# Local attention's scores in 64x64 tiles, and four score products at once for the selected tokens

## The chip, the cores and the metric

The kernel is one program on one core of a Trainium2 chip. Its time is the device time of that core in microseconds, the median of the runs shown. TensorE (PE) multiplies, VectorE (DVE) and ScalarE (ACT) work on its results in PSUM, GpSimd (POOL) prepares small operands, SyncE (SP) issues DMAs.

## The reference

Six layers follow each other: a gated feed-forward layer, linear attention, the feed-forward layer again, a layer that joins local attention and attention of selected tokens ("route" below), latent attention, and the route layer once more. The change is in the route layer, which runs twice, on 8 batches of 256 tokens, 128 features, 8 heads of 64:

```python
light = local_attn(_ln(x), Wqkv, Wout_l)   # windows of 64 tokens; a window sees itself and its two neighbours
sim = jnp.where(valid, sim, -1e9)          # the first and the last window have one neighbour
sq, iq = route(x, rt_q, 64)                # the 64 best tokens of a batch as queries
skv, ikv = route(x, rt_kv, 128)            # the 128 best as keys
heavy = heavy_attn(x[iq], x[ikv], skv, ...)  # 8 heads over 128 keys and one null key with its null value
out = null_q everywhere, heavy at iq
return out + light
```

All matrix products are in float32, except small ones in bfloat16 that add a mask or a maximum.

## The kernel before, in words

Each engine has its own program, written out by hand, and semaphores join them. In the route layer a first part does local attention for all batches, with the router's iterations on DVE beside it, and a second part does the selected tokens.

**Local attention.** Batch b goes through four quarters, one for each pair of heads. The PE loop is a Python loop over b from -1 to 8 and written out in full. In each quarter PE does `turned_scores(b, pair)` (keys as rows, queries as columns, for the exponential by ACT), a projection of a later batch (`project_qk`), `scores(b + 1, pair)` (queries as rows, from which DVE takes the maximum in `top`), and the products with the values (`values`, `summed`) or `project_out`. A half h holds two windows. `scores` writes 128 queries x 192 keys for each half and each of the pair's two heads, with the 64 features of a head as contraction, so two heads stand above each other on PE's rows (64x128 tiles). A product with one row (`g_row`, `g_neg`) then adds -1e9 to the 64 columns that one of the two windows may not see. `turned_scores` does the same with keys and queries exchanged, and a bfloat16 product with `marks` adds the negative maximum and the mask. `scores(b, pair)` waits until DVE has taken the maximum of the pair before (`mx`), `turned_scores` until ACT has read the pair before (`p`). A projection waits until the one before last has been copied out of its bank (two banks, `input_bank`); q is copied by DVE, k and v by ACT. In a quarter DVE's queue has `normalised`, `copy_q` and `scale_z` where there is one, `top`, and up to four router steps, in this order.

**Selected tokens.** `heavy(b)` runs once for each batch; the six middle ones are a loop of the hardware over two bodies (`batches`). PE: `heavy_scores(b)`, `heavy_turn_out(b - 1)`, `gather(b + 1)`, `spread_slots(b)`, `heavy_project_out(b - 1)`, `heavy_turn(b)`, `project_k(b + 1)`, `put_back(b - 1)`, `project_q(b + 1)`, `heavy_values(b)`, `project_v(b + 1)`. `heavy_scores` takes all 128 rows: `h_q[j]` has zeros in the other head's rows. `heavy_values` does head side 0, then head side 1, each with a product of 4 rows that brings the null value in. DVE: `pick(b + 1)`, the maximum, `h_back` (a comparison of the spread slots with a row number), `pick_row`, copies, the reciprocal, `add_heavy(b - 1)`, `copy_heavy_q(b + 1)` in two halves, `token_stats(b - 1)`, and the product of values and reciprocal. `heavy_turn_out(b)` needs the latter (`ho`), and also ACT's copy of v (`hv`).

## Time and profile before

| | |
|---|---|
| median of 3 runs | 1091.48 us (1088.66 to 1154.73) |
| the profiled execution | 1089.49 us, span 1087.7 us |
| mean granted TensorE clock | 0.930 of 2.4 GHz |
| busy share of the span | PE 89%, PEld 64%, DVE 62%, ACT 35%, POOL 13% |
| chain that ended last | PE 70%, DVE 13%, issue 10%, ACT 4% |

The span runs from the first to the last instruction. A float32 product has two records of PE (it goes through the array twice), so x4 in a row is two products. A record's length counts from its start to its modelled end, some of it beside the next record, so the time of a block is read from one group's start to the next one's.

### The profile page before, as it was taken

How to read it: one execution, taken by the hardware profiler on the slowest of the kernel's cores; microseconds unless marked ns; L12 is line 12 of the kernel's file. 1: busy time of each engine (PE TensorE's matmuls, PEld its weight loads, DVE VectorE, ACT ScalarE, POOL GpSimd, SP SyncE). 2: the span in 40 equal slices, each digit the busy share in tenths (PEclk: the TensorE clock that was granted, in tenths of full speed). 3: DMA queues.
4: the chain of work that ended last, by engine and by line, in shares of the span. 5: the costliest groups of instructions: out<-in, count | busy, mean ns of one | idle time of the engine just before them, and what ended most of it. 6: DMA issues, size and time to landing. Idle time of an engine off the chain costs nothing.

```text
span 1087.7 us, 23083 instructions
## 1 busy us (share of the span) xinstructions
PE 966.8 (89%) x8840; PEld 698.3 (64%) x8840; DVE 670.0 (62%) x1914; ACT 381.5 (35%) x913; POOL 141.6 (13%) x289
## 2 busy tenths in 40 slices
PE   3499999899559999999999589999879999999997
PEld 3378888788446666667776245555446667667775
DVE  5778787887664565566555456667453665565553
ACT  3321111111333434333332136667623433333332
POOL 5011111110110000000000254350010000000000
PEclk9889898999689999999999569999979999999997
DMA  5000000000000000000000233322000000000000
GB/s 188 0 2 1 2 0 0 0 0 1 0 1 1 1 2 2 2 2 2 1 0 1 60 86 97 82 75 75 3 1 1 2 1 2 2 2 2 10 10 20
DMA packets 13751, 20.07 MB, mean 18 GB/s; under 512 B 1504, under 2 KB 12128, under 8 KB 12256
## 3 DMA queue, kind: packets, MB, share of 16 engines
q1 hardware_dynamic: 13520, 18.67, 5.9%
q8 instruction: 60, 0.98, 0.4%
q10 hardware_dynamic: 144, 0.20, 0.1%
q14 instruction: 27, 0.22, 0.1%
HBM read 14.53 MB, written 4.19 MB: 17 GB/s over the span
## 4 chain that ended last, share of the span: by engine, by line
PE 70%; DVE 13%; issue 10%; ACT 4%; POOL 2%; DVEq 1%; DMA 1%; SPq 0%; POOLq 0%; ACTq 0%
PE bank L1598 6%; PE bank L1659 6%; PE bank L1627 6%; PE bank L1645 5%; PE bank L1685 3%; PE bank L1605 3%; PE bank L604 3%; PE bank L1083 2%; PE bank L1833 2%; PE bank L1828 2%; PE bank L589 2%; PE bank L1104 2%; PE bank L1631 2%; PE bank L1117 2%; PE bank L1803 2%
## 5 line engine op out<-in xcount | busy, mean ns | idle before, releaser
L1398 DVE TENSOR_REDUCE arena<-bank 128x2 f32<-128x512 f32 x128 | 85.0, 688 | 53.3 <-PE bank L1083 52.2
L2166 DVE TENSOR_REDUCE arena<-bank 128x4 f32<-128x768 f32 x64 | 61.3, 958 | 65.6 <-PE bank L1631 65.6
L1221 ACT ACTIVATE arena<-bank 128x512 f32<-128x512 f32 x128 | 74.5, 594 | 51.0 <-PE bank L1104 50.2
L604 PE MATMUL bank<-arena 128*128 128x9 f32 x512 | 66.2, 257 | 13.4 <-DVE arena L929 7.5
L604 PEld LDWEIGHTS bank<-arena 128*128 128x128 f32 x512 | 65.6, 200 | 16.6 <-issue 8.7
L1627 PE MATMUL bank<-arena 64*128 64x192 f32 x512 | 76.2, 374 | 0.0
L1598 PE MATMUL bank<-arena,w_sb 128*128 128x256 f32 x256 | 74.5, 418 | 1.3 <-ACT arena L1924 1.3
L589 PE MATMUL bank<-arena 128*128 128x128 f32 x512 | 72.1, 289 | 0.3 <-DVE arena L863 0.3
L1945 ACT ACTIVATE arena<-bank 128x768 f32<-128x768 f32 x64 | 51.9, 811 | 55.8 <-PE bank L1649 54.1
L589 PEld LDWEIGHTS bank<-arena 128*128 128x128 f32 x512 | 67.1, 203 | 2.8 <-DVE arena L863 0.3
L1645 PE MATMUL bank<-arena 64*128 64x192 f32 x512 | 66.2, 356 | 0.4 <-ACT arena L1945 0.4
L1598 PEld LDWEIGHTS bank<-arena,w_sb 128*128 128x128 f32 x256 | 46.1, 199 | 19.3 <-issue 12.4
L1659 PE MATMUL bank<-arena 128*32 128x192 f32 (+2 forms) x1536 | 54.5, 274 | 1.2 <-DVE x L2181 1.2
L1083 PE MATMUL bank<-arena 72*128 72x256 bf16 x256 | 52.4, 291 | 1.1 <-DVE arena L1398 1.1
L1659 PEld LDWEIGHTS bank<-arena 128*32 128x32 f32 x1536 | 42.2, 109 | 17.1 <-issue 12.6
L2082 POOL TENSOR_TENSOR arena<-arena,c_sb 128x8 bf16<-128x8 f32 x32 | 9.1, 283 | 332.4 <-issue 295.4
L1645 PEld LDWEIGHTS bank<-arena 64*128 64x128 f32 x512 | 38.8, 185 | 21.0 <-issue 12.5
L1104 PE MATMUL bank<-arena 128*128 128x256 bf16 x256 | 49.5, 277 | 0.5 <-ACT arena L1221 0.4
L2137 DVE SCALAR_TENSOR_TENSOR arena<-arena,c_sb 16x256 f32<-16x256 f32 x98 | 46.2, 471 | 2.5
L1627 PEld LDWEIGHTS bank<-arena 64*128 64x128 f32 x512 | 38.5, 184 | 14.1 <-issue 7.3
L868 DVE TENSOR_TENSOR arena<-bank,c_sb 128x512 f32<-128x512 f32 x64 | 43.8, 684 | 2.8 <-PE bank L589 2.8
L1935 ACT ACTIVATE arena<-bank 128x512 f32<-128x512 f32 x32 | 19.1, 597 | 73.1 <-PE bank L1605 73.1
(297 smaller groups left out, 1978.4 us busy)
## 6 DMA issues: line engine op xcount, KB each, us to landing
arena<-q_dram SPq DMA_DIRECT2D x24, 192.0 KB
arena<-k_dram SPq DMA_DIRECT2D x24, 192.0 KB
w_sb<-w_dram SPq DMA_DIRECT2D x2, 1578.5 KB, 11.0
q_dram<-arena SPq DMA_DIRECT2D x24, 64.0 KB, 2.9
k_dram<-arena SPq DMA_DIRECT2D x24, 64.0 KB, 2.1
x<-x_dram SPq DMA_DIRECT2D x4, 256.0 KB, 4.4
out_dram<-x SPq DMA_DIRECT2D x4, 256.0 KB, 2.3
c_sb<-c_dram SPq DMA_DIRECT2D x1, 601.5 KB, 6.5
```

The source lines that it names most:

```text
L589: ins = pe.matmul(bank[1 + u % 2][:, j * P:(j + 1) * P], l_pkm[parity][:, quad * 4 + j, h * P:(h + 1) * P], l_pqT[parity][:, h * P:(h + 1) ...
L604: ins = pe.matmul(bank[7][:, h * 144 + k * LV:h * 144 + (k + 1) * LV], l_a[:, u % 2, j, :], l_v[parity][:, h * LH + k, :], start=u == 0 an ...
L1083: ins = pe.matmul(bank[s % 2][:, h * T:(h + 1) * T], a_stack[n % 3][0][0:STACK_ROWS, u, h * P:(h + 1) * P], a_stack[n % 3][1][0:STACK_ROWS ...
L1104: ins = pe.matmul(bank[2 + u % 2][:, k * T:(k + 1) * T], a_stack[b % 3][1][:, u, k * P:(k + 1) * P], a_stack[b % 3][0][:, u, :], start=Tru ...
L1221: act.activation(a_pT[:, u % (2 * GROUP), :, :].rearrange("p k t -> p (k t)"), bank[2 + u % 2][:, :], ACT.Exp).then_inc(S["p"], 1)
L1398: dve.tensor_reduce(a_mx[:, i % 2, :, u % GROUP], bank[s % 2][:, :].rearrange("p (h k) -> p h k", h=HALVES), AX_X, ALU.max, negate=True).t ...
L1598: ins = pe.matmul(to[:, j * T:(j + 1) * T], w_sb[:, at:at + P], g_zT[b % 2][:], start=True, stop=True)
L1627: pe.matmul(bank[j][:, h * KEYS:(h + 1) * KEYS], q[rows, pair, h * P:(h + 1) * P], k[rows, pair, h * WIN:h * WIN + KEYS], start=True, stop ...
L1645: pe.matmul(bank[2 + j][:, h * KEYS:(h + 1) * KEYS], k[rows, pair, h * P:(h + 1) * P], q[rows, pair, h * WIN:h * WIN + KEYS], start=True, ...
L1659: ins = pe.matmul(to[u * E_COLS:(u + 1) * E_COLS, out_at:out_at + n], stationary(h, u), g_p[:, 2 * s + u // 2, u % 2, h * KEYS + at:h * KE ...
L1945: act.activation(g_p[:, pair, :, :], two_banks(2)[:, :, 0:SPAN], ACT.Exp).then_inc(S["p"], 1)
L2166: dve.tensor_reduce(g_mx[:, s, :, :, i].rearrange("p h j -> p j h"), two_banks(0)[:, :, 0:SPAN].rearrange("p j (h k) -> p j h k", h=HALVES ...
```

## The change

Local attention: each product covers one window of 64 queries (or keys), and the keys (or queries) it may see, 128 or 192 columns. Windows go in the pairs (0, 3) and (2, 1), with both heads: four products on four 64x64 tiles of PE. The products for the mask are gone; `close_windows` has DVE write -1e9 once in a stage into the places in PSUM that no product writes. `scores(b + 1, pair)` stands directly behind `turned_scores(b, pair)`, ahead of the projections.

Selected tokens: `heavy_scores` takes 64 rows for each head, and in every second pair the heads change sides, so that the products of two successive pairs lie on the four different tiles. `heavy_values` alternates the sides, without the product for the null value; DVE multiplies the null values by their probabilities (`h_null`) and adds them. The slots of `h_back` come from two transposes in `gather` and no longer from `spread_slots`. The loop over batches is written out in full (`unrolled`) on PE, ACT and DVE. Fewer memsets on POOL (`FILLS` 5 for 16), and `marks` and `null_v` are smaller (192 and 256 columns less to load).

```diff
+        WINDOW_PAIRS = ((0, 3), (2, 1))
+
+        def window(n):
+            first, last = max(n - 1, 0) * WIN, min(n + 2, T // WIN) * WIN
+            h = n // 2
+            shift = h * KEYS - h * WIN
+            return slice((n % 2) * WIN, (n % 2 + 1) * WIN), slice(first + shift, last + shift), slice(first, last)
...
-                for h in range(HALVES):
-                    for j in range(2):
-                        rows = slice(j * DH, (j + 1) * DH)
-                        pe.matmul(bank[j][:, h * KEYS:(h + 1) * KEYS], q[rows, pair, h * P:(h + 1) * P],
-                                  k[rows, pair, h * WIN:h * WIN + KEYS], start=True, stop=False, skip_group_check=True)
-                    far = h * KEYS + (KEYS - WIN if h == 0 else 0)
-                    for j in range(2):
-                        ins = pe.matmul(bank[j][:, far:far + WIN], g_row[j * DH:j * DH + 1, h, :],
-                                        g_neg[j * DH:j * DH + 1, :], start=False, stop=True, skip_group_check=True)
+                for windows in WINDOW_PAIRS:
+                    for n in windows:
+                        for j in range(2):
+                            at, cols, seen = window(n)
+                            rows = slice(j * DH, (j + 1) * DH)
+                            ins = pe.matmul(bank[j][at, cols], q[rows, pair, n * WIN:(n + 1) * WIN], k[rows, pair, seen],
+                                            start=True, stop=True, skip_group_check=True)
                 ins.then_inc(S["sc_psum"], 1)
...
-                for h in range(HALVES):
-                    for j in range(2):
-                        rows = slice(j * DH, (j + 1) * DH)
-                        pe.matmul(bank[2 + j][:, h * KEYS:(h + 1) * KEYS], k[rows, pair, h * P:(h + 1) * P],
-                                  q[rows, pair, h * WIN:h * WIN + KEYS], start=True, stop=False, skip_group_check=True)
-                    for j in range(2):
-                        rows = slice(j * DH, (j + 1) * DH)
-                        ins = pe.matmul(bank[2 + j][:, h * KEYS:(h + 1) * KEYS], marks[rows, i, h, :],
-                                        g_mT[s][rows, h * WIN:h * WIN + KEYS], start=False, stop=True,
-                                        skip_group_check=True)
+                for windows in WINDOW_PAIRS:
+                    for n in windows:
+                        for j in range(2):
+                            at, cols, seen = window(n)
+                            rows = slice(j * DH, (j + 1) * DH)
+                            pe.matmul(bank[2 + j][at, cols], marks[rows, i, :], g_mT[s][rows, seen],
+                                      start=True, stop=False, skip_group_check=True)
+                    for n in windows:
+                        for j in range(2):
+                            at, cols, seen = window(n)
+                            rows = slice(j * DH, (j + 1) * DH)
+                            ins = pe.matmul(bank[2 + j][at, cols], k[rows, pair, n * WIN:(n + 1) * WIN], q[rows, pair, seen],
+                                            start=False, stop=True, skip_group_check=True)
                 ins.then_inc(S["st_psum"], 1)
...
                 if now:
                     turned_scores(b, 0)
                 if ahead:
-                    project_qk("q23", b + 1)
+                    scores(b + 1, 0)
                 if now:
                     turn_tops(b, 1)
                 if ahead:
-                    scores(b + 1, 0)
+                    project_qk("q23", b + 1)
...
                 for h in range(HALVES):
-                    ins = pe.matmul(bank[1][:, 0:NKV + NQ], h_y[:, h, :], h_hot[:, h, :],
+                    ins = pe.matmul(bank[1][:, 0:NKV + NQ], h_y[:, h, :], h_hot[:, h, 0:NKV + NQ],
                                     start=h == 0, stop=h == 1)
                 ins.then_inc(S["x_psum"], 1)
+                wait(pe, S["hback"], b)
+                for h in range(HALVES):
+                    ins = pe.transpose(bank[4][0:NQ + 1, h * P:(h + 1) * P], h_hot[:, h, NKV:NKV + NQ + 1], ident)
+                ins.then_inc(S["b_psum"], 1)
                 for h in range(HALVES):
                     ins = pe.matmul(bank[3][:, 0:1], h_hot[:, h, 0:NKV], h_w[:, h, :], start=h == 0, stop=h == 1)
                 ins.then_inc(S["w_psum"], 1)
-
-            def spread_slots(b):
-
-                pe.wait_ge(S["hslot"], b + 1)
-                wait(pe, S["hpT"], 2 * b)
-                pe.matmul(bank[4][0:NQ + 1, 0:T], c("ones", ROUTES)[:, 0:NQ + 1], h_slot[:], start=True, stop=True)\
-                  .then_inc(S["b_psum"], 1)
...
+            def side_of(t, side):
+                return side ^ (t % 2)
+
             def heavy_scores(b):
-                pe.wait_ge(S["kq"], 3 * b + 3)
+                pe.wait_ge(S["kq"], 2 * b + 2)
                 for t in range(PAIRS):
-                    for j in range(2):
-                        ins = pe.matmul(bank[5 + t // 2][j * NQ:(j + 1) * NQ, (t % 2) * 256:(t % 2) * 256 + NKV + 1],
-                                        h_q[j][:, t, :], h_k[:, t, :], start=True, stop=True)
+                    for side in range(2):
+                        half = side_of(t, side)
+                        rows = slice(half * DH, (half + 1) * DH)
+                        ins = pe.matmul(bank[5 + t % 2][side * NQ:(side + 1) * NQ, (t // 2) * 256:(t // 2) * 256 + NKV + 1],
+                                        h_q[rows, t, :], h_k[rows, t, :], start=True, stop=True, skip_group_check=True)
                 ins.then_inc(S["hs_psum"], 1)
             def heavy_turn(b):
                 pe.wait_ge(S["hp"], b + 1)
                 for t in range(PAIRS):
-                    pe.transpose(bank[0][:, t * P:(t + 1) * P], h_p[:, t, 0:NKV], ident)
-                pe.wait_ge(S["hback"], b + 1)
-                pe.transpose(bank[4][0:PAIRS, 0:P], h_p[:, :, NKV], ident).then_inc(S["hpT_psum"], 1)
+                    ins = pe.transpose(bank[0][:, t * P:(t + 1) * P], h_p[:, t, 0:NKV], ident)
+                ins.then_inc(S["hpT_psum"], 1)
             def heavy_values(b):
-                pe.wait_ge(S["hpT"], 2 * b + 2)
+                pe.wait_ge(S["hpT"], b + 1)
                 pe.wait_ge(S["hv"], b + 1)
                 wait(pe, S["x_done"], b)
-                for j in range(2):
-                    rows = slice(j * NQ, (j + 1) * NQ)
-
-                    pe.matmul(bank[7][rows, 0:PAIRS * DH], h_pn[:, rows],
-                              w("null_v", PAIRS)[:, j * 256:(j + 1) * 256], start=True, stop=False,
-                              skip_group_check=True, tile_position=(0, j * NQ))
-                    for t in range(PAIRS):
-                        head = 2 * t + j
+                for t in range(PAIRS):
+                    for side in range(2):
+                        rows = slice(side * NQ, (side + 1) * NQ)
+                        head = 2 * t + side_of(t, side)
                         ins = pe.matmul(bank[7][rows, t * DH:(t + 1) * DH], h_pT[:, t, rows],
-                                        h_v[:, head * DH:(head + 1) * DH], start=False, stop=True,
-                                        skip_group_check=True, tile_position=(0, j * NQ))
+                                        h_v[:, head * DH:(head + 1) * DH], start=True, stop=True,
+                                        skip_group_check=True, tile_position=(0, side * NQ))
                 ins.then_inc(S["ho_psum"], 1)
...
+            def close_windows(i):
+
+                for n in range(2):
+                    at = slice(n * WIN, (n + 1) * WIN)
+                    dve.tensor_scalar(two_banks(i)[at, :, P + n * WIN:P + (n + 1) * WIN],
+                                      c("ones")[at, 0:2 * WIN].rearrange("p (j c) -> p j c", j=2), -BIG, None, ALU.mult)
...
+            def copy_back(b, parity):
+                dve.wait_ge(S["b_psum"], b + 1)
+                dve.tensor_copy(h_back[parity][:], bank[4][0:NQ + 1, 0:T]).then_inc(S["hback"], 1)
...
-                dve.wait_ge(S["b_psum"], b + 1)
-                dve.tensor_scalar(h_back[parity][:], bank[4][0:NQ + 1, 0:T], c("iota_p", NQ + 1), None, ALU.is_equal)\
-                   .then_inc(S["hback"], 1)
-                if not last:
-                    pick_row(b + 1)
                 if not first:
                     heavy_output(b - 1)
                 if not last:
...
                 dve.wait_ge(S["hpT_psum"], b + 1)
                 dve.tensor_copy(h_pT[:].rearrange("p t q -> p (t q)"), bank[0][:, :]).then_inc(S["hpT"], 1)
                 dve.wait_ge(S["hp"], b + 1)
-                dve.reciprocal(h_rec[:], h_sum[:]).then_inc(S["horder"], 1)
+                dve.reciprocal(h_rec[:], h_sum[:])
+                dve.tensor_tensor(h_null[:], w("null_v").rearrange("p (t d) -> p t d", t=PAIRS),
+                                  h_p[:, :, NKV:NKV + 1].to_broadcast([P, PAIRS, DH]), ALU.mult).then_inc(S["horder"], 1)
                 if not first:
                     add_heavy(b - 1)
                 if not last:
+                    copy_back(b + 1, 1 - parity)
                     copy_heavy_q(b + 1)
                 if not first:
                     token_stats(dve, S, b - 1)
-                dve.wait_ge(S["horder"], b + 1)
+                dve.wait_ge(S["horder"], 2 * b + 1)
                 dve.wait_ge(S["ho_psum"], b + 1)
-                dve.tensor_tensor(h_o[:], bank[7][:, 0:256].rearrange("p (t d) -> p t d", t=PAIRS),
-                                  h_rec[:].unsqueeze(2).to_broadcast([P, PAIRS, DH]), ALU.mult).then_inc(S["ho"], 1)
-
-            batches(dve, S, heavy)
+                dve.tensor_tensor(h_null[:], bank[7][:, 0:256].rearrange("p (t d) -> p t d", t=PAIRS), h_null[:], ALU.add)\
+                   .then_inc(S["horder"], 1)
+                dve.wait_ge(S["horder"], 2 * b + 2)
+                dve.tensor_tensor(h_o[:], h_null[:], h_rec[:].unsqueeze(2).to_broadcast([P, PAIRS, DH]), ALU.mult)\
+                   .then_inc(S["ho"], 1)
+
+            unrolled(S, heavy)
```

The other quarters exchange `scores` and `project_qk` in the same way. Not shown: the scales, the packing of weights and constants, and ACT, which no longer copies the null probabilities (`h_pn`).

The order of PE in the first quarter of a steady batch, before (T = `turned_scores` L1645 and L1649, S = `scores` L1627 and L1631, L1598 `project_qk`, L1614 `turn_tops`):

```order
L1645 MATMUL bank<-arena 128x192 x2
L1649 MATMUL bank<-arena,c_sb 128x192 x2
L1645 MATMUL bank<-arena 128x192 x2
L1649 MATMUL bank<-arena,c_sb 128x192 x2
L1598 MATMUL bank<-arena,w_sb 128x256 x2
L1614 MATMUL bank<-arena 128x128 x2
L1627 MATMUL bank<-arena 128x192 x2
L1631 MATMUL bank<-g_neg,g_row 128x64 x2
L1627 MATMUL bank<-arena 128x192 x2
L1631 MATMUL bank<-g_neg,g_row 128x64 x2
```

And in the changed kernel (T is L1654 and L1660, S L1638, `project_qk` L1607, `turn_tops` L1623):

```order
L1654 MATMUL bank<-arena,c_sb 64x128 x4
L1660 MATMUL bank<-arena 64x128 x4
L1654 MATMUL bank<-arena,c_sb 64x192 x4
L1660 MATMUL bank<-arena 64x192 x4
L1638 MATMUL bank<-arena 64x128 x4
L1638 MATMUL bank<-arena 64x192 x4
L1623 MATMUL bank<-arena 128x128 x2
L1607 MATMUL bank<-arena,w_sb 128x256 x2
```

S has moved from behind L1598 and L1614 to directly behind T, and eight groups have become six, all on 64x64 tiles.

PE at the start of the stage, before (L1587 turns z, L1598 x6 is q01, k01 and q23 of batch 0):

```order
L1587 MATMUL bank<-c_sb,arena 128x128 x2
L1598 MATMUL bank<-arena,w_sb 128x256 x6
L1627 MATMUL bank<-arena 128x192 x2
L1631 MATMUL bank<-g_neg,g_row 128x64 x2
L1627 MATMUL bank<-arena 128x192 x2
L1631 MATMUL bank<-g_neg,g_row 128x64 x2
L1598 MATMUL bank<-arena,w_sb 128x256 x2
```

And in the changed kernel (L1596 turns z, L1607 `project_qk`):

```order
L1596 MATMUL bank<-c_sb,arena 128x128 x2
L1607 MATMUL bank<-arena,w_sb 128x256 x4
L1638 MATMUL bank<-arena 64x128 x4
L1638 MATMUL bank<-arena 64x192 x4
L1607 MATMUL bank<-arena,w_sb 128x256 x2
L1638 MATMUL bank<-arena 64x128 x4
```

Between the first S and the second there now stands q23 alone; the projection k23 and z of the next batch come behind the second S.

DVE in a pass over the selected tokens, from the copy of the turned probabilities, before:

```order
L2290 COPY arena<-bank 128x1
L2381 COPY arena<-bank 128x512
L2383 RECIPROCAL arena<-arena 128x4
L2308 ISA
L2308 REGISTER_ALU
L2308 SCALAR_TENSOR_TENSOR x<-bank,arena,x 128x128
L2308 ISA
L2308 REGISTER_ALU
L2308 SCALAR_TENSOR_TENSOR x<-bank,arena,x 128x128
L2296 TENSOR_SCALAR arena<-bank 64x256 x2
L2392 TENSOR_TENSOR arena<-bank,arena 128x256
```

And in the changed kernel (L2378 the same copy, L2381 and L2392 `h_null`, L2310 `add_heavy`, L2289 `copy_back`, L2298 `copy_heavy_q`, L276 `token_stats`):

```order
L2294 COPY arena<-bank 128x1
L2378 COPY arena<-bank 128x512
L2380 RECIPROCAL arena<-arena 128x4
L2381 TENSOR_TENSOR arena<-w_sb,arena 128x256
L2310 SCALAR_TENSOR_TENSOR x<-bank,arena,x 128x128 x2
L2289 COPY arena<-bank 65x256
L2298 TENSOR_SCALAR arena<-bank 128x256
L276 BN_STATS stats<-x 128x6 x2
L2392 TENSOR_TENSOR arena<-bank,arena 128x256
L2395 TENSOR_TENSOR arena<-arena 128x256
```

`copy_back`, which was a comparison at an earlier place, stands behind `add_heavy`; two operations are added, and one of the two halves of `copy_heavy_q` is gone.

## Rows read from the trace of the kernel before

**Rows 1.** The page: busy time by engine, and TensorE's granted clock in 40 slices.

```profile
PE 966.8 (89%) x8840; PEld 698.3 (64%) x8840; DVE 670.0 (62%) x1914; ACT 381.5 (35%) x913; POOL 141.6 (13%) x289
...
PEclk9889898999689999999999569999979999999997
```

**Rows 2.** Windows: stretch, length, busy us of PE, PEld, DVE, ACT, POOL; clock, DMA, GB/s.

```profile
404.40:427.10 22.70, 22.70 (x283) 15.63 (x283) 13.57 (x41) 8.79 (x17) 1.56 (x4) 1.00 0.01 1
543.40:546.80 3.40, 3.40 (x18) 1.80 (x18) 1.85 (x9) 0.69 (x1) 0.00 (x0) 0.50 0.00 0
```

**Rows 3.** Timeline of PE in one steady quarter: start us, us, group, idle before.

```profile
419.85 0.60 PE L1645 MATMUL bank<-arena 64*128 64x192 f32 x4
...
420.89 1.13 PE L1598 MATMUL bank<-arena,w_sb 128*128 128x256 f32 x4
421.95 0.60 PE L1627 MATMUL bank<-arena 64*128 64x192 f32 x4
422.48 0.20 PE L1631 MATMUL bank<-g_neg,g_row 1*128 1x64 bf16 x2
...
423.27 1.16 PE L1685 MATMUL bank<-w_sb,arena 128*128 128x128 f32 x8
...
425.22 0.87 PE L1659 MATMUL bank<-arena 128*32 128x192 f32 x24
426.02 0.43 PE L1645 MATMUL bank<-arena 64*128 64x192 f32 x2
```

**Rows 4.** Timeline of DVE after the next q product of a steady quarter.

```profile
428.24 0.69 DVE L2158 TENSOR_SCALAR arena<-bank 128x512 f32<-128x512 f32 x1 [0.21 <-PE bank L1598]
428.85 0.47 DVE L2152 TENSOR_SCALAR arena<-y_all,scales 128x128 f32<-128x128 f32 x2
429.68 0.96 DVE L2166 TENSOR_REDUCE arena<-bank 128x4 f32<-128x768 f32 x1 [0.36 <-PE bank L1631]
```

**Rows 5.** Timeline of PE at the first scores of the stage.

```profile
322.27 0.60 PE L1627 MATMUL bank<-arena 64*128 64x192 f32 x4
...
324.87 0.60 PE L1627 MATMUL bank<-arena 64*128 64x192 f32 x4
```

**Rows 6.** Timeline of PE in one pass over selected tokens.

```profile
576.36 1.12 PE L1803 MATMUL bank<-w_sb,arena 128*128 128x512 f32 x2
577.42 1.10 PE L1810 MATMUL bank<-arena 128*64 128x129 f32 x16
578.45 0.44 PE L1841 MATMUL bank<-c_sb,arena 128*128 128x128 f32 x2
...
579.82 0.64 PE L1782 MATMUL bank<-arena,c_sb 16*65 16x256 f32 x2
580.39 1.09 PE L1850 MATMUL bank<-w_sb,arena 128*64 128x128 f32 x8
581.41 0.66 PE L1817 MATMUL bank<-c_sb,arena 128*128 128x128 f32 x4
...
584.54 0.61 PE L1828 MATMUL bank<-w_sb,arena 4*64 4x256 f32 x2 [0.18 <-DVE x L2308]
...
586.87 0.70 PE L1803 MATMUL bank<-w_sb,arena 128*128 128x512 f32 x1
```

**Rows 7.** Timeline of DVE in the same pass.

```profile
576.54 0.43 DVE L2392 TENSOR_TENSOR arena<-bank,arena 128x256 f32<-128x256 f32 x1 [1.26 <-PE bank L1833]
...
578.57 0.76 DVE L2366 TENSOR_REDUCE arena<-bank 128x2 f32<-128x258 f32 x2 [0.38 <-PE bank L1810]
...
582.21 0.69 DVE L2381 COPY arena<-bank 128x512 f32<-128x512 f32 x1 [0.35 <-PE bank L1819]
...
583.78 0.61 DVE L2308 SCALAR_TENSOR_TENSOR x<-bank,arena,x 128x128 f32 x2 [0.79 <-PE bank L1858]
...
585.30 0.49 DVE L273 BATCH_NORM_STATS2 stats<-x  x2
```

**Rows 8.** Timeline of ACT in the same pass.

```profile
579.36 0.37 ACT L2028 ACTIVATE arena<-bank,arena 128x129 f32<-128x129 f32 x1
```

89 lines of the change are left out of this document (36 added, 53 removed).

## The prediction

> **What bounds the kernel now.** I read the page first: PE is busy for 89% of the span and the granted clock is full through most of both route stages [rows 1]. Busy PE is not proof, so the windows come next. In a batch of local attention PE is busy for 22.70 of 22.70 us at full clock, DVE for 13.57 and ACT for 8.79 [rows 2]. There PE waits for nobody, and what is taken from its blocks comes off the time until another queue catches up. The timeline of a quarter gives the blocks from start to start: T 419.85 to 420.89, 1.04; a projection P 1.06; S 421.95 to 423.27, 1.32; the values V (x24) 0.80 [rows 3]. In the selected tokens, a pass takes 576.36 to 586.87, 10.51 us, also almost filled by PE [rows 6]; but DVE, ACT and PE hand over to each other there, so the next chain has to be priced too.
>
> **What a block is made of.** At 2.4 GHz and two cycles a float32 column, a column costs 0.83 ns in each of the two records of a product. P then streams 4x256 columns in 0.85 and has 0.21 left for filling and emptying the array; V streams 2x(192+128+64) = 768 columns in 0.64, and 0.16 is left. V has 24 records, so the four tiles of 32 columns must run side by side; in T, four records are two tiles side by side. One half of S up to its mask product takes 421.95 to 422.48, 0.53: 384 columns, 0.32, and again 0.21. So each change of tile shape costs 0.16 to 0.21 [all rows 3]. S as it is pays it four times, since its mask has one row.
>
> **Local attention.** If four 64x64 tiles run side by side, T needs 2x(128+192) float32 columns, 0.53, and 320 bfloat16 columns at one cycle, 0.13; S needs 0.53. With one change of shape for both, 0.16, and 0.03 for bfloat16 products too short to hide the next weights, T and S take 1.38. Before they took 1.04 + 1.32 = 2.36: 0.98 less. Seven batches of a stage have both, in four quarters: 28 x 0.98 = 27.4. In the fourth quarter the projection now also stands beside `project_out` with the same shape, one change less: 7 x 0.2 = 1.4. The last batch has T alone: 4 x 0.2 = 0.8. The bounds of the 1.38 are 1.35 with no handover and 2.6 with the tiles two by two (a rival below); I take the low side, since V's rows show four tiles at once.
>
> What is late next? DVE's queue. A batch of PE shrinks from 22.7 to some 18.6, and DVE's 13.57 [rows 2] still fits into it. But its order is fixed: in the first quarter `copy_q` 0.61, `scale_z` 0.47 and `top` 0.96 follow each other behind the projection q23 [rows 4]. The first quarter (T and S, the turn, P, and two V of 0.80 less one change of shape) is now about 4.0. The tight place is S of the second quarter: q23 comes 1.38 + 0.15 + 1.06 + 0.13 = 2.7 after the quarter's start (0.15 for two short transposes, 0.13 from PE's block to DVE's start, both estimates by the starts of rows 3 and 4), the maximum at 2.7 + 0.61 + 0.47 + 0.96 = 4.7, and PE arrives there at 4.0 + 0.7 = 4.7. I take no wait; 0.5 each time would be 3.5 us a stage, which the range holds.
>
> The start of a stage pays. PE's second S now stands behind q23 alone. The first S starts at 322.27 as before [rows 5], since it waits for k01 either way; S alone is 0.53 + 0.16 = 0.7, so q23 comes at 322.27 + 0.7 + 1.06 + 0.13 = 324.2. DVE does `copy_q` and `scale_z` ahead of `top`: 324.2 + 2.04 [rows 4] = 326.2. Before, that S started at 324.87 [rows 5]. Behind it k23 (1.06) must be copied by ACT (0.6) before v0 has its bank, with only z's 0.2 in between, where 1.5 of other work stood: v0 is 2.6 later. The third and fourth S give 0.6 each back, so the start costs 1.4 instead of gaining 2.4. The wait of v0 comes once more in batch 0, which has no V there: 0.5. Another 0.2 is lost in the last batch, where T waits for ACT. The four fills of `close_windows` are in DVE's idle time while PE projects q01; they are small beside the 0.61 of a copy, and at most 1 us a stage if that cover is gone. POOL's shorter chain is not waited for.
>
> Local attention: 27.4 + 1.4 + 0.8 - 1.4 - 0.5 - 0.2 = 27.5 a stage, 55 in both.
>
> **Selected tokens, PE's part.** `heavy_values` is 584.54 to 586.87, 2.33: two null products and two blocks that share no time. After: 2x4x64 columns of one side at 0.83, 0.43, the other beside it, and 0.16: 0.6. `heavy_scores` goes from 1.03 to 2x2x129 columns, 0.43, plus 0.16, 0.6. `spread_slots` 0.57 goes, the two transposes cost about 0.23, and the null transpose goes, 0.11 (one of five equal parts of its block). In sum 10.51 - 1.73 - 0.43 - 0.57 + 0.23 - 0.11 = 7.9 [rows 6].
>
> But after that PE no longer sets the pass. I put 0 where `heavy_values` ends (576.36). DVE adds at 0.18 (0.43) and, after a semaphore, multiplies; I take 0.35, the 0.43 of the row less an overlap such as the one now: 1.0. `pick` takes from 576.97 to 578.19, where the maximum's idle 0.38 begins: 1.2, so 2.2. Two maxima 0.76 [rows 7]: 3.0. ACT's four exponentials of 0.37 each, 1.5, and a handover [rows 8]: 4.6. PE turns; the copy starts 582.21 - 581.41 - 0.11 = 0.7 later and takes 0.6 until the next: 5.9. Reciprocal and null product 0.5: 6.4. `add_heavy` starts now at 583.78, 2.37 after the turn; without the null transpose and some 0.3 of register steps in front of it that is 6.6. It takes 0.61: 7.2. `copy_back` and the one half left of `copy_heavy_q` 0.42 each, like the 0.43 of the same 256 columns, and `token_stats` 0.45: 8.5, where the values have been waiting since 8.0. A pass is 8.5 - 0.18 = 8.3; I take 8.4, DVE's chain being the bound, and 7.9 to 9.0 as its bounds.
>
> Six full intervals of 10.5 become 8.4, 12.6; the first interval gives 2; the last pass has shorter values and one addition more, 1.5; the entry saves one half of `copy_heavy_q`, 0.4. That is 16.5 a stage, 33 in both. The written-out loops are more code, priced at nothing: local attention is written out already, and PE does not wait in it [rows 2]. 192 columns less of constants may give 0.5 at the start.
>
> **The sum.** 55 + 33 + 0.5 = 88.5. The profiled execution took 1089.49, so 1001 there; it was 2.0 under the median of 1091.48, which gives 1003.
>
> **A page on the tiles.** That row and column tiles also combine is shown by no row here. The Trainium skill, "TensorE: Matmul & The Clock Gate", Part 3, states that they compose and that each further tile costs about 4 ns of start; by that the sum stands. The Trainium skill, "TensorEngine Tiling (Array Packing)", Gotcha 2, says column tiling excludes Fast Weight Load; the bfloat16 `marks`, 128 columns until now, would then load more slowly, by my estimate 0.03 twice in T, 4 us in all. By it the time would be 1007; no row has such a load, and I keep 1003.
>
> **The rivals.** *The clock or the handovers eat the second part.* Once in a stage the clock falls to half for 3.4 us in the selected tokens, out of a stretch that PE filled (543.40) [rows 2]; half of 3.4 is 1.7 lost. With PE idle for half a microsecond or more in each pass, it may fall once a pass: six more, 10 us a stage, 1023. For it: the fall at full load; against it: local attention has none.
>
> *Two tiles at a time.* If a row tile and a column tile exclude each other, T and S take 2 x 1.2 + 0.2 = 2.6, 0.2 more than now: 6 us a stage lost, while the values, with column tiles only, still give nearly all of the 33: 1091.5 - 33 + 12 = 1070, on the edge of what can be told. Against it: both kinds run side by side in these rows.
>
> *Slower: one tile at a time.* If products on 64x64 tiles run one after another, T and S take 4 x 1.2 + 0.2 = 5.0, 2.6 more in 56 pairs: 146, less the 33, 1205. It decides from where T and S together exceed 2.36 + 33/56 = 2.95, which is when fewer than about 1.7 of the four tiles overlap. Only the absence of a row for the combined shape speaks for it.
>
> *DVE bounds local attention.* The tight place above waits 1 us a batch, and others follow: 10 us a stage, 1023 too.
>
> **How the numbers follow.** Forecast 0.74, by itself 985 to 1016 (passes of 7.9 to 9.0: 6 either way; handovers in T and S: 4; 0.5 a quarter of waits: 7). Clock or handovers 0.11, DVE in local attention 0.08, two tiles 0.04, one tile 0.03. To hold 8 in 10 the range takes in the cases at 1023: 985 to 1028. A measurement of this kernel tells about 2% from no change. Faster by more than that: 0.93 (the first three cases); within it 0.04 (two tiles); slower 0.03.
>
> **What the new profile would show.** L1654 and L1660 followed by L1638 with four records starting within 0.03 and 1.4 from T's start to the projection; a steady batch near 18.7; PE idle for about 2 near the first scores of each stage, ended by DVE's maximum; passes of 8.4, with PE's waits ended by DVE. I am wrong if records of 64*64 start one after the other, or if DVE's maximum stops PE in every batch.

## The result, and the profile after

The changed kernel takes 1001.68 us (median of 4 runs, 991.75 to 1008.94) against 1098.13 for the kernel before (4 runs, 1088.66 to 1154.73). The ratio is 0.912, with a 95% interval of 0.897 to 0.927. The forecast was 1003, the range 985 to 1028. The profiled execution took 998.15, its span is 996.4.

The page of the changed kernel, as in [rows 1]:

```profile
PE 861.9 (87%) x9784; PEld 641.6 (64%) x9784; DVE 662.8 (67%) x1922; ACT 375.0 (38%) x897; POOL 138.3 (14%) x267
...
PEclk9889899889868999999999658999997999999998
```

PE has 105 us less work in 944 more matmuls, and DVE 7 us less. The windows, as in [rows 2]: two batches of the steady local attention, and one pass over selected tokens.

```profile
399.00:417.50 18.50, 18.50 (x354) 13.58 (x346) 13.39 (x42) 8.68 (x17) 1.59 (x5) 1.00 0.01 3
417.50:436.00 18.50, 18.50 (x355) 13.60 (x349) 12.89 (x41) 8.38 (x16) 1.59 (x5) 1.00 0.01 3
523.30:531.49 8.19, 8.00 (x80) 6.41 (x79) 5.75 (x25) 3.49 (x12) 0.00 (x0) 1.00 0.00 0
```

A batch is 18.5 where it was 22.7, PE is still busy all the time, and a pass is 8.19 where it was 10.51. The timeline of PE through the first quarter of a batch, which answers to [rows 3]:

```profile
417.50 0.25 PE L1654 MATMUL bank<-arena,c_sb 64*64 64x128 bf16 x4
417.58 0.39 PE L1660 MATMUL bank<-arena 64*64 64x128 f32 x8
417.81 0.25 PE L1654 MATMUL bank<-arena,c_sb 64*64 64x192 bf16 x4
417.89 0.49 PE L1660 MATMUL bank<-arena 64*64 64x192 f32 x8
418.21 0.71 PE L1638 MATMUL bank<-arena 64*64 64x128 f32 x16
418.86 0.29 PE L1623 MATMUL bank<-arena 128*128 128x128 bf16 x2
...
421.45 0.25 PE L1654 MATMUL bank<-arena,c_sb 64*64 64x128 bf16 x4
...
422.17 0.39 PE L1638 MATMUL bank<-arena 64*64 64x128 f32 x8
```

T starts at 417.50 (`marks` L1654, then the scores L1660), S (L1638) at 418.21, and the turned tops at 418.86: T and S together take 1.36 (predicted: 1.38; before: 2.36). The S of the second quarter starts at 422.17 with no idle time ahead of it, which was the tight place of the prediction. The maximum that it waits for had ended in time, by the timeline of DVE:

```profile
421.10 0.95 DVE L2161 TENSOR_REDUCE arena<-bank 128x4 f32<-128x768 f32 x1
421.97 0.47 DVE L2132 SCALAR_TENSOR_TENSOR arena<-arena,c_sb 16x256 f32<-16x256 f32 x1
```

The start of the stage answers to [rows 5]. PE's timeline there, with the idle time of each S at the end of its row:

```profile
328.08 0.78 PE L1638 MATMUL bank<-arena 64*64 64x128 f32 x16 [0.78 <-ACT arena L1937]
...
331.95 0.78 PE L1638 MATMUL bank<-arena 64*64 64x128 f32 x16 [2.04 <-DVE arena L2161]
...
334.48 1.12 PE L1614 MATMUL bank<-w_sb,arena 128*128 128x512 f32 x2 [0.47 <-ACT arena L1937]
...
335.97 0.78 PE L1638 MATMUL bank<-arena 64*64 64x128 f32 x16
...
339.46 0.78 PE L1638 MATMUL bank<-arena 64*64 64x128 f32 x16 [1.09 <-DVE arena L2161]
```

The wait of some 2 us was forecast, and the one of v0 behind it. The wait of 1.09 ahead of the fourth S was not. DVE's timeline shows where it comes from: the third maximum (L2161) stands behind the copy of q01 (L2153), and that product now comes after the third S.

```profile
337.85 0.69 DVE L2153 TENSOR_SCALAR arena<-bank 128x512 f32<-128x512 f32 x1 [3.07 <-PE bank L1607]
338.45 0.95 DVE L2161 TENSOR_REDUCE arena<-bank 128x4 f32<-128x768 f32 x1
```

**Where the time came from.** I mark the same events in every profile's timeline of PE, all in the first route stage (the second agrees within 0.15 except where a stretch at half clock falls into its start, in e4, e9 and e10; e5_two_quarters has one in the start of both stages). "Start" is from the first S to the first T, "local" from there to the first `gather`, "passes" from the first to the last record of `heavy_scores`. The last two columns are the moment at which the stage's first matmul (the turned z) starts, and the time of the profiled execution.

```
                    start   local  passes | stage begins    time
before              11.98  175.16   75.04 |  316.22     1089.49
changed kernel      14.44  144.94   56.64 |  322.28      998.15
e1_unrolled         11.98  175.17   72.04 |  321.28     1087.22
e2_local            14.45  144.96   72.04 |  319.42     1031.13
e3_selected         11.98  175.16   56.67 |  323.45     1055.08
e4_in_turn          14.54  152.31   56.66 |  316.42     1009.34
e5_two_quarters     19.50  181.96   56.67 |  327.39     1085.62
e6_start_pe          9.64  144.95   56.65 |  330.49     1001.75
e7_start_dve        11.25  144.98   56.66 |  320.11      987.77
e8_own_bank         14.45  144.96   56.66 |  319.85      996.27
e9_pick_early       14.45  144.95   54.96 |  329.97     1006.13
e10_pick_bank       14.44  144.96   53.49 |  324.92      994.02
e11_old_order        9.65  150.33   56.66 |  322.04      999.77
e12_best             9.65  144.95   53.47 |  328.89      990.14
```

A stage gives 30.2 in its local part, loses 2.5 at its start, gives 18.4 in the passes and 2.3 to 2.6 behind the last of them; with the turned z and `gather`, which together gave 0.4 in the first stage and took 0.2 in the second, that is 48.8 in the first and 48.6 in the second, 97.4. The profiles differ by 91.3, because the part ahead of the first stage, whose instructions are the same, took 6.06 longer (316.22 to 322.28). The column shows that this is chance: over 14 profiles whose instructions up to there are the same it runs from 316 to 330. This is why I read most of the experiments by their stages. The prediction's 88.5 stands against 91.3 and 97.4. Its 0.5 for the smaller constants is not to be seen: the first product of PE starts at 12.85 in both profiles.

### The profile page after: what moved, and what is told of

Its sections match the earlier page's. It is cut to its first block, busy times and chain, and to the rows that moved or that the text cites. A ratio compares the mean times of both kernels' runs of the same rounds, so it can differ in the third digit from the quotient of the medians.

```text
span 996.4 us, 24622 instructions
## 1 busy us (share of the span) xinstructions
PE 861.9 (87%) x9784; PEld 641.6 (64%) x9784; DVE 662.8 (67%) x1922; ACT 375.0 (38%) x897; POOL 138.3 (14%) x267
## 4 chain that ended last, share of the span: by engine, by line
PE 66%; DVE 15%; issue 11%; ACT 5%; POOL 2%; DMA 1%; DVEq 1%; SPq 0%; ACTq 0%; POOLq 0%
PE bank L1607 7%; PE bank L1669 7%; PE bank L1638 4%; PE bank L1660 3%; PE bank L607 3%; PE bank L1614 3%; PE bank L1695 3%; PE bank L1086 3%; PE bank L592 2%; PE bank L1107 2%; PE bank L1120 2%; PE bank L1857 2%; PE bank L1654 2%; PE bank L1810 2%; PE bank L1796 1%
## 5 line engine op out<-in xcount | busy, mean ns | idle before, releaser
L1224 ACT ACTIVATE arena<-bank 128x512 f32<-128x512 f32 x128 | 74.5, 594 | 51.1 <-PE bank L1107 50.3
L607 PEld LDWEIGHTS bank<-arena 128*128 128x128 f32 x512 | 66.8, 203 | 15.3 <-issue 9.0
L1607 PE MATMUL bank<-arena,w_sb 128*128 128x256 f32 x256 | 74.7, 417 | 1.3 <-ACT arena L1931 1.3
L592 PEld LDWEIGHTS bank<-arena 128*128 128x128 f32 x512 | 68.1, 205 | 4.1 <-DVE arena L866 1.3
L2161 DVE TENSOR_REDUCE arena<-bank 128x4 f32<-128x768 f32 x64 | 60.7, 949 | 10.7 <-PE bank L1638 10.6
L1607 PEld LDWEIGHTS bank<-arena,w_sb 128*128 128x128 f32 x256 | 45.6, 198 | 19.3 <-issue 12.8
L2153 DVE TENSOR_SCALAR arena<-bank 128x512 f32<-128x512 f32 x32 | 22.1, 691 | 51.7 <-PE bank L1607 51.7
L1638 PE MATMUL bank<-arena 64*64 64x128 f32 (+1 forms) x1024 | 46.2, 297 | 8.0 <-DVE arena L2161 6.3
L1660 PE MATMUL bank<-arena 64*64 64x128 f32 (+1 forms) x1024 | 51.2, 295 | 0.0
L1120 PE MATMUL bank<-arena 128*32 128x256 f32 x512 | 41.9, 389 | 0.1
L1638 PEld LDWEIGHTS bank<-arena 64*64 64x64 f32 x1024 | 31.0, 132 | 13.9 <-DVE arena L2161 7.5
```

The lines of the kernel that those rows point to most:

```text
L592: ins = pe.matmul(bank[1 + u % 2][:, j * P:(j + 1) * P], l_pkm[parity][:, quad * 4 + j, h * P:(h + 1) * P], l_pqT[parity][:, h * P:(h + 1) ...
L607: ins = pe.matmul(bank[7][:, h * 144 + k * LV:h * 144 + (k + 1) * LV], l_a[:, u % 2, j, :], l_v[parity][:, h * LH + k, :], start=u == 0 an ...
L1120: ins = pe.matmul(bank[4 + g // 2][j * VCOLS:(j + 1) * VCOLS, (g % 2) * T:(g % 2 + 1) * T], a_v[b % VDEEP][:, u, k, :], a_pT[:, u % (2 * G ...
L1224: act.activation(a_pT[:, u % (2 * GROUP), :, :].rearrange("p k t -> p (k t)"), bank[2 + u % 2][:, :], ACT.Exp).then_inc(S["p"], 1)
L1607: ins = pe.matmul(to[:, j * T:(j + 1) * T], w_sb[:, at:at + P], g_zT[b % 2][:], start=True, stop=True)
L1638: ins = pe.matmul(bank[j][at, cols], q[rows, pair, n * WIN:(n + 1) * WIN], k[rows, pair, seen], start=True, stop=True, skip_group_check=True)
```

## The experiments

**The loop written out, alone.** On the kernel before:

```diff
-            batches(pe, S, heavy)
+            unrolled(S, heavy)
```

(and the same on ACT and DVE).

> The kernel before with one edit: the passes over the selected tokens are written out on TensorE, ScalarE and VectorE in place of the loop (nothing else of the change). Theory A (the loop's register instructions stood on the path, some 0.2 us of a pass): first to last scores of the selected tokens in the first stage falls from 74.2 us to 72 to 73, the program by 2 to 5 us. Rival: they ran beside other work, and the 74.2 us stay within 0.4, apart from one half-clock window worth 1.6.

(The 74.2 and the 56.2 of the expectations end where the last `heavy_scores` starts, those of the table where its last record starts.) The passes fell from 75.04 to 72.04. Of the 3.0, 1.6 is a half-clock window that the profile before has in its passes (intervals of 11.34 and 11.29 among those of 10.50 to 10.53) and this one has not; each pass is 10.28, 0.22 to 0.23 shorter, which is 1.4. So theory A holds in its size: written out, a pass is shorter by what was expected. Which instruction of the loop it was, no run tells. In the time of the whole kernel this can't be told: 1087.22 against 1087.05 for a run of the kernel before beside it. The prediction priced these loops at nothing.

**Local attention alone.** The kernel before, with `scores`, `turned_scores`, `close_windows`, the new order and the loop written out.

> The kernel before with the local attention of the changed kernel (64x64 tiles, the scores ahead of the projections, the closed blocks written once by VectorE) and the passes written out, but with the old products of the selected tokens. If the two halves of the change act apart, the first stage shows the changed kernel's 144.9 us from the first turned scores to the first gather (175.2 before) and the first scores to the first turned scores at 14.4 us (12.0 before), with the selected tokens where e1_unrolled has them: some 1091 - 56 = 1035 us, give or take the 6 us by which the unchanged stages differ between profiles. If the halves depend on each other, the passes or the gather move too.

1031.13. Start and local part are those of the changed kernel to 0.02 (14.45 and 144.96), the passes those of e1_unrolled. The halves add up.

**Selected tokens alone.**

> The changed kernel's selected tokens (written out, four products at once, values in alternating halves, null value on VectorE) with the old local attention. Theory: first to last scores at 56.2 us as in the changed kernel (74.2 before), last scores to the next stage 17.9 (20.6), local attention at 175.2 from its first turned scores to the gather as before; some 1090 - 42 = 1048 us, give or take 6. If it is the smaller part, as the ledger of the prediction had it (33), about 1057.

Passes 56.67, local part 175.16, start 11.98. The time is 1055.08, some 7 above the expectation, and the stage began 7.2 later than in the profile before: the halves are as the theory has them, at 27.8 a stage for the local attention and 20.8 for the selected tokens, the half-clock window's 1.6 among these.

**The same tiles, neighbours on the same quarter.**

```diff
-        WINDOW_PAIRS = ((0, 3), (2, 1))
+        WINDOW_PAIRS = ((0, 2), (1, 3))
...
-                    for n in windows:
-                        for j in range(2):
+                    for j in range(2):
+                        for n in windows:
```

> The changed kernel, with the same 64x64 products, the same count of matmuls and columns, but written in an order in which neighbours use the same quarter of the array: the two windows that share a quarter stand one after the other (pairs 0,2 and 1,3, half j in the outer loop). Counted in columns that pass one after the other this makes 768 of 320. Theory (the gain of local attention is that four quarters run side by side): a block of turned scores and scores takes 2.4 to 3.3 us instead of 1.36, and the time from the first turned scores to the gather rises from 144.9 us by 29 to 54, to or over the 175.2 of the kernel before. Rival (the gain is in fewer columns, no mask products and no 128-row shape, and the order of the quarters does not matter): 1.36 and 144.9 stay.

The two windows of a pair now share rows of a bank, and the shift of the first one's turned scores would be lost by the second's `start=True`; only the time is read. (The Trainium skill, "PSUM — Partial Sum Buffer", section "PSUM: the matmul accumulator", has such a start clear the accumulation state of the whole bank for its rows; no profile shows this.) Expected were 2.4 to 3.3 for a block. The timeline of PE:

```profile
424.44 0.33 PE L1654 MATMUL bank<-arena,c_sb 64*64 64x128 bf16 x4
...
425.14 0.27 PE L1638 MATMUL bank<-arena 64*64 64x128 f32 x1
425.17 0.27 PE L1660 MATMUL bank<-arena 64*64 64x128 f32 x1
425.20 0.27 PE L1638 MATMUL bank<-arena 64*64 64x128 f32 x1
...
425.28 0.27 PE L1660 MATMUL bank<-arena 64*64 64x128 f32 x1
...
426.02 0.48 PE L1607 MATMUL bank<-arena,w_sb 128*128 128x256 f32 x1
```

**Only two quarters.** This one does.

```diff
-            return slice((n % 2) * WIN, (n % 2 + 1) * WIN), slice(first + shift, ...
+            return slice(0, WIN), slice(first + shift, ...
```

> The changed kernel with one edit: every 64x64 product of the local attention writes output rows 0 to 63, so that only the two quarters of the array under these columns are used, with the same matmuls in the same order and the same number of columns in all (scores and weights of the windows 1 and 3 then land on those of 0 and 2 and the other 64 rows keep old numbers: this is for its time alone). Theory (the gain of local attention comes from four quarters that run side by side, each with its own quarter of the columns): a quarter that is left has twice the columns, a block of turned scores and scores takes 2.5 to 2.7 us instead of 1.36, first turned scores to gather 144.9 + 28 x 1.14 to 28 x 1.34 = 177 to 182, over the kernel before's 175.2. Rival (the blocks are held by the issue of matmuls and weight loads, whose count is the same): within 2 us of 144.9.

```profile
429.15 0.30 PE L1654 MATMUL bank<-arena,c_sb 64*64 64x128 bf16 x4
429.29 0.60 PE L1660 MATMUL bank<-arena 64*64 64x128 f32 x8
429.74 0.33 PE L1654 MATMUL bank<-arena,c_sb 64*64 64x192 bf16 x4
429.90 0.81 PE L1660 MATMUL bank<-arena 64*64 64x192 f32 x8
430.55 1.25 PE L1638 MATMUL bank<-arena 64*64 64x128 f32 x16
431.73 0.48 PE L1607 MATMUL bank<-arena,w_sb 128*128 128x256 f32 x1
```

The instructions and the columns are the same as in the changed kernel, and T and S take 429.15 to 431.73, 2.58 in place of 1.36. The local part is 181.96, inside 177 to 182 and above the 175.16 of the kernel before. So four quarters do run side by side, and all of the gain of local attention hangs on it: on two of them this part is slower than with the old products. (The edit also leaves only 64 rows of PSUM to write to; whether the quarters or these rows set the 2.58, it does not tell apart.) It also gives the size of the prediction's rival "two tiles at a time" (2.6).

**The start of the stage, from PE's side.** In the batch ahead of the first alone, PE's old order (q23, S, k23, z, S, ...):

```diff
+                if b < 0:
+                    project_qk("q23", b + 1)
                 if ahead:
                     scores(b + 1, 0)
...
-                if ahead:
+                if ahead and b >= 0:
                     project_qk("q23", b + 1)
```

(and so for the other three).

> The changed kernel, with TensorE's order of the kernel before in the batch ahead of the first (q23 ahead of the first scores, k23 and the turned z ahead of the second, q01 and the turned tops ahead of the third, k01 ahead of the fourth), the changed order in all others. Theory (the start of the stage lost what the new order put behind the scores: two waits of 2.04 and 1.09 us for VectorE's max, which stands behind a copy of q that now comes later): from the first turned z to the first turned scores 20.2 to 20.5 us become 15.6 to 17 (18.0 before), the rest of the stage stays; 7 to 9 us of the program. Rival (PE waits there for the projections' copies on ScalarE in either order): 19 to 20.5.

From the turned z to the first T it is 15.99 in the first stage (6.35 + 9.64) and 16.39 in the second, against 20.24 and 20.46: 4.3 and 4.1 less, as expected. No S waits any more. The time of the profiled execution is 1001.75 all the same: the stage began at 330.49, 8.2 later than in the changed kernel's profile, which is the chance of the column above.

**The start, from DVE's side.**

```diff
+                if b < 0:
+                    top(b + 1, 0)
                 if ahead:
                     copy_q("q23", b + 1)
                     if ahead2:
                         scale_z(b + 2)
-                    top(b + 1, 0)
+                if ahead and b >= 0:
+                    top(b + 1, 0)
```

(and so for `top(b + 1, 2)` and the copy of q01).

> The changed kernel, with two maxima moved on VectorE in the batch ahead of the first: that of the first pair ahead of the copy of q23 and the scaling of z, that of the third ahead of the copy of q01; TensorE's order as changed. Theory as for e6_start_pe, mended from the other side: of the waits of 2.04 and 1.09 us some 1.5 to 1.9 and 0.8 to 1.0 go, first turned z to first turned scores 17.4 to 18.2 us. Rival (another wait, for ScalarE's copy of k or of z, is right behind them): over 19.

17.13 and 16.87, a little better than expected. PE's timeline at the second and the fourth S:

```profile
327.84 0.78 PE L1638 MATMUL bank<-arena 64*64 64x128 f32 x16
...
334.19 0.78 PE L1638 MATMUL bank<-arena 64*64 64x128 f32 x16
```

Both waits for DVE are gone. The two runs show the cause from both sides: the maximum stood in DVE's queue behind copies whose products the new order had put later.

**What bounds a pass.** The chain of the work that ended last, in the changed kernel, goes through PE and the copy of the values on ACT, and not through DVE:

```profile
515.21 0.70 ACT arena L2030
515.91 0.04 issue
515.95 0.44 PE bank L1848 x2
516.39 0.02 issue
516.41 0.92 PE bank L1781 x4
```

So after this profile I held the prediction's step "DVE's chain sets the pass" for refuted, since DVE even idles for 1.92 at one place in each pass. I gave the turned output a bank of its own, so that PE need not wait for ACT's copy:

```diff
-                    ins = pe.transpose(bank[2][:, n * P:(n + 1) * P],
+                    ins = pe.transpose(bank[0][:, n * P:(n + 1) * P],
...
                 if not first:
-                    pe.wait_ge(S["hv"], b + 1)
                     heavy_turn_out(b - 1)
...
                 if not first:
+                    pe.wait_ge(S["hv"], b + 1)
                     heavy_project_out(b - 1)
```

> The changed kernel, with the turned output of the selected tokens in bank 0, which is free there, in place of bank 2, so that TensorE waits for ScalarE's copy of the values only ahead of the output projection. Theory (a pass of 8.19 us is TensorE's work and this copy of 0.70 in one chain, VectorE has slack): the wait of 0.18 goes and a pass is TensorE's work end to end, 8.05 to 8.10; first to last scores 56.64 becomes 55.7 to 56.0. Rival, the step of the prediction (VectorE's chain sets the pass): 56.6 stays, and TensorE's wait moves to another place, ended by VectorE.

Passes 56.66, not 55.7: the rival held. PE's timeline, and below it the last operations of DVE ahead of the maximum:

```profile
512.78 0.67 PE L1822 MATMUL bank<-arena 64*64 64x129 f32 x16
513.39 0.44 PE L1848 MATMUL bank<-c_sb,arena 128*128 128x128 f32 x2
514.09 0.92 PE L1781 MATMUL bank<-arena 128*128 128x192 f32 x4 [0.27 <-DVE arena L2283]
```

```profile
513.76 0.28 DVE L2283 TENSOR_SCALAR arena<-y_all,scales 128x128 f32<-128x128 f32 x1
513.95 0.75 DVE L2368 TENSOR_REDUCE arena<-bank 128x2 f32<-128x258 f32 x2
```

The wait of 0.18 for ACT is gone, and `gather` now waits visibly for the last operation of `pick`. I took this for two chains of one length, and tested that next. `pick`, 1.23 us of DVE (515.04 to 516.27 in the changed kernel), was moved one pass ahead into DVE's idle time:

```diff
-                if not last:
+                if first:
                     pick(b + 1)
                 dve.wait_ge(S["hs_psum"], b + 1)
...
+                if b + 2 < S["last"]:
+                    dve.wait_ge(S["w_psum"], b + 2)
+                    pick(b + 2)
```

> The changed kernel, with VectorE's eight operations that make the selection matrices of the next batch (1.24 us, between the normalised output and the max) moved one pass ahead, into the 1.92 us in which VectorE waits for the output projection. Theory after e8_own_bank (two chains of the same length set a pass: TensorE's work with ScalarE's copy of the values, and VectorE's chain from the add through the null value and the selection matrices to TensorE's gather): shortening VectorE's alone gains nothing, first to last scores 56.5 to 56.7, TensorE's wait of 0.18 for ScalarE stays. Rival (VectorE's chain alone sets the pass, and the wait for ScalarE is only passed on): 55.9 or less.

Passes 54.96, so my theory fell again and its rival held: 7.91 a pass in place of 8.19, with ACT's 0.18 still there. DVE's chain alone had set the pass. PE's timeline shows where that was hidden; here are the changed kernel (first) and e9:

```profile
524.14 0.44 PE L1848 MATMUL bank<-c_sb,arena 128*128 128x128 f32 x2 [0.18 <-ACT arena L2030]
524.60 0.92 PE L1781 MATMUL bank<-arena 128*128 128x192 f32 x4
525.36 0.38 PE L1786 MATMUL bank<-c_sb,arena 128*65 128x128 f32 x2
```

```profile
523.03 0.44 PE L1848 MATMUL bank<-c_sb,arena 128*128 128x128 f32 x2 [0.18 <-ACT arena L2030]
523.31 0.82 PE L1781 MATMUL bank<-arena 128*128 128x192 f32 x4
523.96 0.38 PE L1786 MATMUL bank<-c_sb,arena 128*65 128x128 f32 x2
```

From the turned output to `gather` are 0.46 against 0.28, and from `gather` to the next group 0.76 against 0.65: together 0.29, the 0.28 of the pass. The first part lies under the modelled end of the record ahead, and the second is the first weight load of `gather`, which could not start early since it was the one that waited (it starts at 524.60 with its product; in e9 at 523.20, 0.11 ahead of it). Neither counts as idle, so the chain named only ACT. In the changed kernel's DVE timeline the last operation ahead of that load ends at 524.55:

```profile
524.27 0.28 DVE L2283 TENSOR_SCALAR arena<-y_all,scales 128x128 f32<-128x128 f32 x1
```

**Both.**

> e8_own_bank and e9_pick_early together. Theory (two chains of the same length): both are shortened now, TensorE's work alone sets the pass, 8.05 to 8.10 us in place of 8.19, first to last scores 55.7 to 56.0 in place of 56.6. Rival (something else stands at 8.19): 56.6.

7.66 a pass, passes 53.49; that is below the 8.05 to 8.10, which I had worked out from PE's groups with the hidden waits in them. Against 8.19 it is 0.53: the 0.29 at `gather`, and 0.24 between `heavy_scores` and the turned output (0.61 from start to start for 0.85 in e9), of which the profile shows only 0.18 as idle. The window of one pass:

```profile
509.13:516.80 7.67, 7.67 (x80) 6.39 (x79) 5.84 (x24) 3.49 (x12) 0.00 (x0) 1.00 0.00 0
```

PE is busy all the time now. The four runs make one table of a pass: 8.19 as changed, 8.19 with the bank, 7.91 with `pick` ahead, 7.66 with both. DVE's chain is 8.19, that of PE and ACT is 7.91, PE's own work is 7.66.

**The order, alone.** The small tiles kept, PE's old order in all batches.

> The changed kernel, with TensorE's order of the kernel before throughout the local attention (each block of scores behind the projection that used to stand ahead of it), the 64x64 tiles kept. By the prediction's terms: a block of turned scores and a block of scores no longer stand together, one change of shape more for each pair of blocks (0.16 to 0.21 us by 28) and the last quarter's: first turned scores to gather 144.9 + 4.5 to 7.3 = 149.5 to 152.2; the start of the stage as in e6_start_pe, 4.2 shorter. So a stage is within 0.3 to 3 us of the changed kernel's, longer, and the order by itself is worth nearly nothing of the 91 us. Rival (the order was what let the small tiles pay: with a projection in front, TensorE waits for VectorE's max as it did not): over 155.

Start 9.65, local part 150.33 (expected: 149.5 to 152.2). A stage, from the turned z to the last scores, is 226.43 against 225.99 of the changed kernel (227.62 against 226.16 in the second). So the tiles alone give 175.16 - 150.33 = 24.8 in the local part and 2.3 at the start; the new order gives 5.4 and takes 4.8 back. In PE's timeline S stands by itself again, and takes 0.71 up to the next group in place of 0.65:

```profile
421.65 0.78 PE L1638 MATMUL bank<-arena 64*64 64x128 f32 x16
422.36 0.87 PE L1669 MATMUL bank<-arena 128*32 128x192 f32 x24
```

**Everything that helped.** PE's old order in the batch ahead of the first, the bank, and `pick` one pass ahead.

> e6_start_pe and e10_pick_bank together: TensorE's order of the kernel before in the batch ahead of the first alone, the turned output in its own bank, the selection matrices made one pass ahead. By the three profiles, against the changed kernel: 4.2 us of each start, 3.15 of each stage's passes, 14.7 in all: some 983 to 987 us, 0.895 to 0.90 of the kernel before, the changed kernel having 0.912. Rival (the unchanged stages' half-clock windows swallow it): no lower than 995.

989.26 us (6 runs, 982.80 to 993.29) against 1093.69 (12 runs), ratio 0.904, 95% interval 0.900 to 0.907. By its stages it has what was expected: 218.57 and 219.06 from the turned z to the last scores, against 225.99 and 226.16, 14.5 in both. The time is above the 983 to 987 and the ratio above the 0.895 to 0.90 that were expected, and its interval lies inside that of the changed kernel (0.897 to 0.927, from four runs), so the whole times alone don't tell the two apart; the rows of the stages do.

## Why the prediction was right

**The bound of local attention: right.** PE was busy throughout before and after, and T + S came out at 1.36 for 1.38. e5_two_quarters shows the mechanism. The sum of the local part was 27.4 + 1.4 + 0.8 - 0.5 - 0.2 = 28.9 and is 30.2. e11_old_order puts 5.4 of it on the order, for which my terms had 5.9 (28 x 0.16 + 1.4); the tiles gave 24.8, for which they leave 23.0. Of these 1.8 more, 0.6 is the 1.36 in place of 1.38. In the last batch the 0.2 for T's wait for ACT should not have been taken off, since the kernel before has this wait too (0.20 there, 0.23 now). The rest I have not traced.

**The tight place: right.** No S of a steady quarter waits for DVE, at the 0.1 us of slack that its rows show (421.10 + 0.95 against 422.17).

**The start of the stage: right mechanism, one wait missed.** 1.4 was the loss, 2.46 is what it costs. The step "The third and fourth S give 0.6 each back" failed: I followed DVE's queue to the second S only, and the same thing happens once more, 1.09 ahead of the fourth.

**Selected tokens: "DVE's chain being the bound" was right, and the size nearly so.** 8.3 was worked out, 8.4 taken, 8.19 measured; e9_pick_early and e10_pick_bank show it. "PE's part" was 7.9 and is 7.66: the 0.22 of the loop is missing in it, the step that the prediction priced at nothing. The first interval gave 2.4 for 2, the stretch behind the start of the last scores 2.7 for 1.5, the entry 0.1 for 0.4. Together a stage gave 20.8 for 16.5, of which 1.6 is the half-clock window that only the profile before had, so 19.2 is what the change gives.

**The sign that I had named failed.** "Passes of 8.4, with PE's waits ended by DVE": the wait that the profile shows is ended by ACT, and by this sign I would have discarded a right step. Only the experiments undid that.

**The rivals.** Two tiles at a time, and one at a time, are excluded by e5_two_quarters, so row and column tiles do combine; the row of four `marks` records at 417.50 is 0.25 long, where one record by itself takes 0.24. The slower weight loads of `marks`, by which the time would have been 1007, do not show in the 1.36. The clock does not fall in the passes of the changed kernel (8.18 to 8.19 each, in both stages). DVE does not bound local attention.

**The total: near partly by chance.** The selected tokens gave 2.7 a stage more than forecast, the local attention 0.3, and a half-clock window 1.6; that would have made some 97; 6 us of slower clock ahead of the stages took most of that back. The 1003 also starts from 1091.48 for the kernel before, whose median is 1098.13 with its fourth run; by the two medians the change gave 96.5, and that 1003 met 1001.68 so closely is luck.

## What to carry to other kernels

Count the columns for each quarter of the array: here products of 64x64 took about the time of the fullest quarter, and they paid only while all four were filled. When an order is changed for the steady part, follow every queue that waits for it through the first and the last batch as well; here the start gave back nearly all that the order had gained. And before a chain is believed, compare the same group in a run where the suspect is early: a wait that ends just behind another one's, or that falls on a weight load, stands in no idle column.

## What was not expected of the hardware

- The part ahead of the first stage, the same in all kernels, takes 316 to 330 us. The granted clock over it (seventh value of a window) goes with it, here the kernel before, the changed kernel and e9:

```profile
60.00:300.00 240.00, 213.94 (x1443) 188.25 (x1442) 185.99 (x479) 49.02 (x150) 31.47 (x28) 0.90 0.00 0
```

```profile
60.00:300.00 240.00, 216.72 (x1425) 189.29 (x1424) 181.36 (x464) 47.03 (x145) 31.50 (x27) 0.88 0.00 0
```

```profile
60.00:300.00 240.00, 218.93 (x1393) 189.32 (x1391) 175.88 (x448) 43.79 (x136) 29.80 (x24) 0.85 0.00 0
```

They begin the stage at 316.22, 322.28 and 329.97. PE has idle time in this part and the clock falls there now and then, in a different place each time; why it does in one run more often than in another stays open.
